# Four Flamingo-style gated layers on one core: x normalised once and turned by a diagonal product in the prelude, weight scales of the last layer folded into the weights

## The reference

```python
x = x + jnp.tanh(g_xattn[0]) * _L0_xattn_ref(_layernorm(x, axis=-1), ctx_4096, mask, ...)   # 32 heads of 128
x = x + jnp.tanh(g_ffn[0]) * _L0_ffn_ref(_layernorm(x, axis=-1), ...)
...
x = x + jnp.tanh(g_ffn[3]) * _L3_ffn_ref(_layernorm(x, axis=-1), ...)
```

```python
def _dynamic_quant(x, inv_smooth):
    xs = x.astype(jnp.float32) * inv_smooth
    scale = jnp.maximum(jnp.max(jnp.abs(xs), axis=-1, keepdims=True) / QMAX, 1e-08)
    return jnp.clip(jnp.round(xs / scale), -QMAX, QMAX), scale
qg, sg = _dynamic_quant(x_flat, inv_gate)      # x_flat is bf16, 1024 x 512
qu, su = _dynamic_quant(x_flat, inv_up)
gate_out = (qg @ w_gate.T) * sg * s_wgate[None, :]          # 256 columns
up_out = (qu @ w_up.T) * su * s_wup[None, :]
inter = jnp.clip(jax.nn.silu(gate_out) * up_out, -10, 10).astype(jnp.bfloat16)
qi, si = _dynamic_quant(inter, inv_inter)
out = (qi @ w_down.T) * si * s_wdown[None, :]
```

## Time and profile before

| what | value |
|---|---|
| three timed runs | 1664.83, 1665.88, 1668.33 us (median 1665.88) |
| the profiled execution | 1662.29 us, its span 1660.3 us |
| PE busy | 1584.1 us, 95% |
| DVE busy | 1004.5 us, 60% |
| ACT busy | 734.7 us, 44% |
| POOL busy | 411.3 us, 25% |
| mean granted clock of PE | 0.988 |

### The profile page before, as it was taken

How to read it: one execution, slowest core, us unless ns; L and a number is a source line. 1 busy time by engine, 2 the same in 40 slices (tenths; PEclk the granted TensorE clock), 3 DMA queues, 4 the chain that set the end, 5 groups by cost and what they waited for, 6 DMA issues and landing times.

```text
span 1660.3 us, 25939 instructions
## 1 busy us (share of the span) xinstructions
PE 1584.1 (95%) x8932; PEld 1266.5 (76%) x8932; DVE 1004.5 (60%) x2654; ACT 734.7 (44%) x2125; POOL 411.3 (25%) x271
## 2 busy tenths in 40 slices
PE   8899999999999999999989999999999999999875
PEld 6688888888888888888866869687876797655454
DVE  6763563626636265462876756657485767455787
ACT  4342443424434244442433544536272322677742
POOL 4231320313203132031215100000002533355452
PEclk9999999999999999999999999999999999999998
DMA  5110111101111111111242000000004213000001
GB/s 174 52 42 29 55 41 51 41 28 54 45 47 41 30 64 42 38 46 43 69 173 84 13 13 0 0 13 0 1 14 163 93 51 92 14 14 14 1 0 51
DMA packets 34145, 76.18 MB, mean 46 GB/s; under 512 B 5536, under 2 KB 18336, under 8 KB 31904
## 3 DMA queue, kind: packets, MB, share of 16 engines
q1 hardware_dynamic: 34080, 75.36, 13.5%
HBM read 73.25 MB, written 2.10 MB: 45 GB/s over the span
## 4 chain that ended last, share of the span: by engine, by line
PE 76%; DVE 13%; ACT 3%; issue 3%; DVEq 2%; POOL 1%; DMA 1%; POOLq 0%; SPq 0%; ACTq 0%
PE banks L1098 10%; PE banks L1023 9%; PE banks L1048 9%; PE banks L1031 9%; PE banks L1248 9%; PE banks L1352 5%; PE banks L1154 3%; PE banks L1137 3%; PE banks L1324 3%; PE banks L1476 2%; PE banks L1462 2%; PE banks L1144 2%; PE banks L1483 2%; PE banks L1455 2%; PE banks L1272 1%
## 5 line engine op out<-in xcount | busy, mean ns | idle before, releaser
L516 POOL TENSOR_TENSOR w_q<-w_raw_q,w_q 128x1792 fp32r<-128x1792 f32 x16 | 65.3, 4081 | 484.3 <-ACT w_q L706 484.3
L1098 PE MATMUL banks<-w_o,atT 128*128 128x512 f32 x720 | 180.2, 396 | 0.0
L1048 PE MATMUL banks<-w_v,cT 128*128 128x512 f32 x768 | 178.5, 393 | 0.0
L1023 PE MATMUL banks<-cT,w_k 128*128 128x512 f32 x720 | 178.0, 396 | 0.0
L1031 PE MATMUL banks<-xT,w_q 128*128 128x512 f32 x672 | 164.2, 395 | 5.4 <-DVE qT L1721 2.8
L1048 PEld LDWEIGHTS banks<-w_v,cT 128*128 128x128 f32 x768 | 145.4, 190 | 30.3
L1764 DVE TENSOR_TENSOR sA<-banks,pbias 128x512 f32<-128x512 f32 x64 | 44.1, 688 | 186.5 <-PE banks L1137 185.8
L1098 PEld LDWEIGHTS banks<-w_o,atT 128*128 128x128 f32 x720 | 132.0, 188 | 25.7
L1023 PEld LDWEIGHTS banks<-cT,w_k 128*128 128x128 f32 x720 | 131.9, 188 | 25.5
L1031 PEld LDWEIGHTS banks<-xT,w_q 128*128 128x128 f32 x672 | 123.6, 188 | 31.4 <-DVE qT L1721 3.2
L732 ACT ACTIVATE sA<-sA,nmA 128x128 f32<-128x128 f32 x256 | 99.5, 393 | 60.3 <-DVE nmA L1769 59.9
(11 more groups left out here) (266 smaller groups left out, 3291.2 us busy)
## 6 DMA issues: line engine op xcount, KB each, us to landing
w_raw_k<-in_w0k SPq DMA_DIRECT2D x16, 512.0 KB, 3.3
w_raw_v<-in_w0v SPq DMA_DIRECT2D x8, 1024.0 KB, 4.8
w_raw_q<-in_w0q SPq DMA_DIRECT2D x16, 512.0 KB, 3.3
w_raw_o<-in_w0o SPq DMA_DIRECT2D x15, 512.0 KB, 3.3
cTp<-in_ctxT SPq DMA_DIRECT2D x12, 512.0 KB, 4.0
wq_raw<-in_wq SPq DMA_DIRECT2D x1, 3072.0 KB, 11.3
wo<-in_wo SPq DMA_DIRECT2D x1, 3072.0 KB, 21.0
c_raw<-in_ctxT SPq DMA_DIRECT2D x4, 512.0 KB, 6.9
```

The source lines that it names most:

```text
L516: pool.tensor_tensor(w_part[slot][1][:], w_raw[slot][:], w_part[slot][0][:].bitcast(F32), ALU.subtract).then_inc(S(f"w{slot}_lo"), 1)
L1023: mm = pe.matmul(dst, wk_[l][:, c, h * P:(h + 1) * P], cT[r][:, c, half * HT:(half + 1) * HT], start=c == 0 and n == 0, stop=c == DC - 1 a ...
L1048: mm = pe.matmul(dst, cT[l][:, c, b * P:(b + 1) * P], wv_[r][:, c, :], start=n == 0, stop=n == 3 * DC - 1)
L1098: mm = pe.matmul(dst, atT[l][:, h, t], w[r][:, h, :], start=n == 0, stop=n == 5)
```

## The change

In the prelude:

- x_res is normalised in place, once, with `rstd` (the eight operations of L1675 write x_res, those of L1712 are gone). The further factor of the double norm, now `rr` = (var / (var + eps) + eps)^(-1/2), goes onto the diagonal of a 128 x 128 matrix for each block (`diag`, eight small operations on ACT, from POOL's `rr`), and `turn_x` multiplies the block by it instead of transposing it against the identity.
- There are three stage buffers for four blocks (the fourth takes the first one again), and POOL makes the low part of four operands, DVE of three.
- POOL waits for the eight normalisations before it splits w_q.
- The first keys start in smaller pieces: w_k's low part by quarters, the first chunk of the context by halves.

In the last feed-forward layer:

- The scales of the gate, up and down weights (sd3 with the gate in it) are multiplied into the weights themselves, by six POOL operations in the units 2 to 7 of pair 0 of the last attention layer. The sigmoid takes its input from PSUM with the row's scale, and DVE multiplies PSUM, scale and sigmoid in one operation each. `f3_gates` and its buffer are gone.
- The clip of the codes stands in `f3_round`, behind a drain, in place; `f3_clip` is gone. f3_turn(0) moves ahead of the last projection of the attention layer.
- The products add to x_res on DVE directly; `yd` and POOL's adds are gone.
- The hardware loops over the turns on PE, ACT and DVE are written out.

```diff
@@ SP
-            sp.wait_ge(S("x_split"), 2 * NPAIR)
+            sp.wait_ge(S("x_split"), NPAIR)
+            sp.wait_ge(S("x_split2"), NPAIR)
@@ POOL
-            split("k", 0)
+            pool.wait_ge(S("wk_hi"), 1)
+            for c in range(DC):
+                t = slice(c * 2 * P, (c + 1) * 2 * P)
+                pool.tensor_tensor(w_part["k"][1][:, t], w_raw["k"][:, t], w_part["k"][0][:, t].bitcast(F32),
+                                   ALU.subtract).then_inc(S("wk_lo"), 1)
             split("v", 0)
             pool.wait_ge(S("a_var"), 1)
+            pool.tensor_tensor(rstd[:], ve[:], neg_half[:], ALU.pow).then_inc(S("a_rstd"), 1)
+            pool.wait_ge(S("a_var"), 2)
             pool.tensor_tensor(rr[:], ms[:], neg_half[:], ALU.pow).then_inc(S("a_rstd"), 1)
-            pool.tensor_tensor(rstd[:], ve[:], neg_half[:], ALU.pow).then_inc(S("a_rstd"), 1)
+            pool.wait_ge(S("xr_ready"), NB)
             split("q", 0)
             for k in range(NPAIR):
                 t = slice(k * P, (k + 1) * P)
-                pool.wait_ge(S("x_hi"), k + 1)
-                pool.tensor_tensor(xT[1][:, XT1:, :, t], stage[k % 2][:, XT1:], xT[0][:, XT1:, :, t].bitcast(F32),
-                                   ALU.subtract).then_inc(S("x_split"), 1)
+                pool.wait_ge(S("x_prep"), NPAIR + k + 1)
+                pool.tensor_tensor(xT[1][:, X22:, :, t], stage[k][:, X22:], xT[0][:, X22:, :, t].bitcast(F32),
+                                   ALU.subtract).then_inc(S("x_split2"), 1)
...
+                if i == 0 and 2 <= u < 2 + DC + IC3:
+                    c = u - 2
+                    if c == 0:
+                        pool.wait_ge(S("f3_ws"), 1)
+                    if c < DC:
+                        pool.tensor_tensor(wg3[:, c, :], wg3[:, c, :], sgu3[:].rearrange("p w n -> p (w n)"), ALU.mult)
+                    else:
+                        pool.tensor_tensor(wd3[:, c - DC, :], wd3[:, c - DC, :], sd3[:], ALU.mult)
+                if i == 1 and u == 0:
+                    pool.drain().then_inc(S("f3_ws"), 1)
@@ ACT
+            def diagonal(k):
+                for b in (k, k + NPAIR):
+                    e = act.activation(diag[:, b, :], ident[:], ACT.Copy, scale=rr[:, b:b + 1])
+                e.then_inc(S("x_prep"), 1)
+
+            store_v(0, bank(0), K_UNITS + 1)
+            act.wait_ge(S("const_ready"), 1)
+            act.wait_ge(S("a_rstd"), 2)
+            diagonal(0)
+            store_v(1, bank(1), K_UNITS + 2)
+            for k in range(1, NPAIR):
+                diagonal(k)
...
-                    act.wait_ge(S("f3_g"), 2 * i + j + 1)
-                    act.activation(eg[:, j, :], gu[:, j, 0, :], ACT.Sigmoid).then_inc(S("f3_e"), 1)
+                    act.wait_ge(S("f3_gu"), 2 * i + j + 1)
+                    act.activation(eg[:, j, :], bank(4 + j)[:, 0:I3], ACT.Sigmoid, scale=xsc[:, i, j, 0:1])\
+                        .then_inc(S("f3_e"), 1)
@@ PE
             def turn_x(k):
                 for j, b in enumerate((k, k + NPAIR)):
+                    if j == 0:
+                        pe.wait_ge(S("x_prep"), k + 1)
                     pe.wait_ge(S("xr_ready"), 2 * k + j + 1)
                     if k > 0:
                         pe.wait_ge(S("xw_ready"), 3 * (k - 1) + j + 1)
                     for c in range(DC):
-                        mm = pe.transpose(bank(4 + j)[:, c * P:(c + 1) * P], xr[:, b, c * P:(c + 1) * P], ident[:])
+                        mm = pe.matmul(bank(4 + j)[:, c * P:(c + 1) * P], x_res[:, b, c * P:(c + 1) * P], diag[:, b, :],
+                                       start=True, stop=True)
                     mm.then_inc(S("xr_used"), 1)
...
+                f3_turn(0)
                 x3_project(NPAIR - 1, 1, 0, G3)
...
             def f3_gate_up(i):
-                if not (isinstance(i, int) and i == 0):
-                    pe.wait_ge(S("f3_g"), 2 * i)
-                for j in range(2):
+                for j in range(2):
+                    if i > 0:
+                        pe.wait_ge(S("f3_g"), 2 * i + j - 1)
@@ DVE
             for b in (b for k in range(NPAIR) for b in (k, k + NPAIR)):
-                dve.tensor_scalar(xr[:, b, :], x_res[:, b, :], mv[:, b, 0:1], rr[:, b:b + 1], ALU.subtract,
+                dve.tensor_scalar(x_res[:, b, :], x_res[:, b, :], mv[:, b, 0:1], rstd[:, b:b + 1], ALU.subtract,
                                   ALU.mult).then_inc(S("xr_ready"), 1)
...
             def rows_sums(k):
-                x = stage[k % 2]
-                if k >= 2:
-                    dve.wait_ge(S("x_split"), 2 * k - 1)
+                x = stage[k]
+                if k == NPAIR - 1:
+                    dve.wait_ge(S("x_split2"), 1)
...
-            dve.wait_ge(S("a_rstd"), 2)
-            for b in range(NB):
-                dve.tensor_scalar(x_res[:, b, :], x_res[:, b, :], mv[:, b, 0:1], rstd[:, b:b + 1], ALU.subtract, ALU.mult)
-            dve.drain()
...
                         dve.tensor_scalar(qs[:, i, j, w, :], xs[:, j, w, :], rsc[:, j, w:w + 1], ROUND, ALU.mult, ALU.add)
+                dve.drain()
+                for j in range(2):
+                    for w in range(2):
+                        dve.tensor_scalar(qs[:, i, j, w, :], qs[:, i, j, w, :], ROUND + QMAX, ROUND - QMAX, ALU.min, ALU.max)\
+                           .then_inc(S("f3_q"), 1)
...
             def f3_swiglu(i):
-                dve.wait_ge(S("f3_e"), 2 * i + 2)
-                dve.tensor_tensor(sg[:], eg[:], gu[:, :, 0, :], ALU.mult)
+                for j in range(2):
+                    dve.wait_ge(S("f3_e"), 2 * i + j + 1)
+                    dve.scalar_tensor_tensor(out=sg[:, j, :], in0=bank(4 + j)[:, 0:I3], scalar=xsc[:, i, j, 0:1],
+                                             in1=eg[:, j, :], op0=ALU.mult, op1=ALU.mult)
                 dve.drain()
-                dve.tensor_tensor(sg[:], sg[:], gu[:, :, 1, :], ALU.mult)
+                for j in range(2):
+                    dve.scalar_tensor_tensor(out=sg[:, j, :], in0=bank(4 + j)[:, I3:2 * I3], scalar=xsc[:, i, j, 1:2],
+                                             in1=sg[:, j, :], op0=ALU.mult, op1=ALU.mult).then_inc(S("f3_g"), 1)
                 dve.drain()
...
-                    dve.scalar_tensor_tensor(out=yd[:, j, :], in0=bank(6 + j), scalar=isc[:, i, j:j + 1], in1=sd3[:],
-                                             op0=ALU.mult, op1=ALU.mult).then_inc(S("f3_yd"), 1)
+                    dve.scalar_tensor_tensor(out=x_res[:, 2 * i + j, :], in0=bank(6 + j), scalar=isc[:, i, j:j + 1],
+                                             in1=x_res[:, 2 * i + j, :], op0=ALU.mult, op1=ALU.add).then_inc(S("res"), 1)
```

116 lines of the change are left out of this document (46 added, 70 removed).

## The result

The changed kernel took 1650.64 us (median of 4 runs, 1649.8 to 1654.09) beside 1666.34 us for the kernel before on the same chip (4 runs, 1664.83 to 1668.33): a ratio of 0.9909, 95% interval 0.9891 to 0.9927. It is faster by 0.9%, or 15.7 us, where 8.7 were forecast: at the lower end of the predicted range (1650 to 1664) and 6.6 us under the predicted time. The profiled execution took 1650.53 us with a span of 1648.8; that of before had a span of 1660.3.

The account below looks back on a forecast made before the run. TensorE (PE), busy 95% of the span, was taken as the bound, so only its idle time could yield gains. Prelude -2.9, x3 +2.9 and +1.7, f3 -10.4 gave -8.7 us: 1653.6, plus 3.6 carried over, 1657.2; range 1650 to 1664.

Parts of the forecast that it names:

- rival 1: f3: PE is the new bound, 8.74 us of work per turn; sum only -2.8, 1663.1 us; chance 0.08.
- rival 5: f3 runs at the lower clock throughout, two PE-bound turns cost about +13 us: 1670; chance 0.07.
- PE is full but for two gaps: Last attention layer (x3): PE idles only in gaps of 1.67 and 2.90 us, ended by a DVE copy.
- The weight products on POOL: x3, pair 0: six products, 7.6 us in all, have cover enough and cost 0; at worst +1.3 to +2 us.
- (c): Prelude pipeline: third buffer shortens the loop from 6.8 to 5.9 us per block; query products start 1.5 us earlier, near 55.6.
- Rival 3: Prelude: wider POOL block and w_q split hold DVE back, query products start at 57; gain 0, 1660.1 us; chance 0.08.
- The port: Prelude: DVE and POOL hold each other up without a semaphore; the third buffer notwithstanding, this keeps the pipeline in line.
- (d): Prelude: no second normalisation of x_res, so 42 query matmuls run without the 2.79 us wait, about 10.0 us; gain 3.1 us.
- (b): Prelude: turning x by a product instead of a transposition, +0.8 us per turn_x, +3.2 us of PE.
- rival 4: Prelude: turning by products costs four times a transposition, 4.1 us instead of 1.03; 1658.7 us; chance 0.05.
- The diagonals: Prelude: eight small ACT operations, about 0.3 us each by estimate, 2.4 us in all; first pair due at 26 us.
- Rival 2: The clock stays up at three new places (-3.4 us) and in f3's last down product; 1652 to 1653.8 us; chance 0.12.

Follow-up runs that it names:

- e8: e3 with ACT's sigmoid ahead of the copy of the codes and 11 identity products on TensorE before the last codes; 1643.39 us, ratio 0.9881.
- e5: The changed kernel with two stage buffers instead of three, its two separate counts kept; 1653.17 us (one run).
- e10: The kernel before with DVE's and POOL's splits of x counted by two semaphores instead of one; 1661.11 us (one run).
- e7: The kernel before with one wait more: POOL splits w_q only after DVE's eight normalisations; 1662.86 us (one run).
- e12: e9 with POOL's share of the split of x narrowed from 1024 to 768 columns and 11 identity products before the query products, not 18; 1637.46 us, ratio 0.9831.
- e6: The changed kernel with 18 identity products on TensorE in its idle time before the query products; 1648.31 us, ratio 0.9907.
- e1: The kernel before with the change's prelude edits alone; 1658.34 us, ratio 0.9963.
- e11: e10 with the wait of e7 as well; 1661.59 us (one run).
- e3: The changed kernel with the last two maxima, scales, rounding and clip of x3's pairs 0 and 1 moved behind the copy of y; 1644.35 us, ratio 0.9882.
- e9: The changed kernel with e3, e6 and e8 joined, 13 identity products at x3's start, four weight roundings moved out of the last pair; 1638.94 us, ratio 0.9837.

## Right and wrong, point by point

**f3, right, and 1.4 us better than its sum.** Predicted were swiglu(1) at 1619.8, swiglu(2) at 1627.0, swiglu(3) at 1635.7 behind a sigmoid that waits in ACT's queue, and codes at 1641.3. The rows say 1619.17, 1626.53, 1634.94 with `[1.46 <-ACT eg L982]` before it, 1640.08; the last down product ran at the lower clock as forecast. Chain, order of queues and sizes held. e8 then showed that ACT's order delayed the last sigmoid as the reading said (1.2 us). How much each edit of f3 (gates, clip, POOL's additions, the loops written out) is worth by itself is read from the rows; no run takes them apart. PE as the bound (rival 1) didn't come: of the loop's three turns only one, that of 1629.58, has no idle time ahead of gate and up, as the schedule had it. Nor did rival 5: the lower clock reached only the end.

**x3, the gaps right, the clock right only on average.** +4.6 predicted; the profiled pair shows +3.2, and over all kernels that have the changed stage as it is (196.8, 197.4, 196.9, 196.8) and that of before (193.7, 192.6, 192.9, 191.8, 193.9) the means are 197.0 and 193.0, +4.0. The gaps came out at 3.18 and 4.42 (predicted 3.1 and 4.35), +3.0 for +2.9, with the lower clock behind the first. But the stage as a whole held 20.5 us of lower clock before and 17.1 in the changed kernel, so in the profiled pair the clock took 1.7 us off where +1.7 was forecast; over the same two groups of kernels it is 17.9 and 15.0 us, which comes to +1.5. The other 1.9 us of the +3.2 aren't taken apart; `f3_turn(0)`, 1.97 us of PE's work, now stands inside the stage, where PE waited 0.82 us. The reading that PE is full but for two gaps was wrong: before also has 3.32 us at the start of the stage, 1.92 us at another copy of y (1493.29) and 6.3 us in the last pair, where 10.2 of the 20.5 us of lower clock lie. The weight products on POOL (1.26 to 1.45 us each) cost nothing that a row shows.

**Prelude, the sum right, its reason wrong.** Predicted -2.9, shown -2.9 at x3 (-3.2 to the scores). The step that failed is (c): "the third buffer takes the turning out of this loop". e5 shows it to be worth nothing once the counts are separate, e10 that separate counts in the kernel before give the same 3.1 us to the scores without it, e7 that the wait of POOL gives 1.0. The 6.8 us loop of before held a wait of 2.51 us for POOL that its own timeline shows; I worked out the loop's length and not what ended DVE's idle time in it. The new sum (DVE 1.77, ACT 1.70, POOL 2.41) gave 5.9, and 5.8 is right, because the chain really goes through POOL: a block's own sums are held up by POOL's operation on the block ahead. That this chain is longer than it need be (5.28 with the narrower share, e10 and e12) I took as given. Rival 3 had that half: the wider block holds DVE back, by 2 us until the query products, but not so far that they start at 57.

The port (the way into SBUF that DVE and POOL share by the prediction): on this the row and the Trainium skill (SBUF — State Buffer, Who interferes with whom) agree. It says that a DVE operation with two inputs in SBUF and a GpSimd operation that reads SBUF exclude each other for a whole instruction, whoever was first; L1718 took 2.34 and 2.31 us beside POOL's L516 and L534, and 0.42 alone.

The smaller terms: (d) the query products ran in one piece, 12.17 us at the lower clock and 10.12 in e6 at full clock, predicted 10.0 plus 1.7. (b) A turn costs 1.95 to 2.05 us against 1.03, twice and not four times, so rival 4 fell. The Trainium skill (TensorE: Matmul & The Clock Gate, Terms) has the transposing mode four times faster for FP32; here the rows give 1.9 to 2.0, and they decide. The diagonals took 0.29 us from one to the next, 1.86 for six, and PE waited 0.56 us for the first.

**The clock, right in its places.** The idle time ahead of the query products (4.62 us) and that at y (3.18 us) were followed by the lower clock, as forecast; e6 shows for the first of them that it goes when PE isn't idle. It took 6.8 us there, not 3.4, of which 4.4 fall on the products; it costs 2.0 us and not 1.7. Rival 2 (clock up at the new places) is out, though the measured time would have spoken for it: 1650.6 lies nearer to its 1652 to 1653.8 than to the forecast. The rows decide here, not the number.

**Basis, the rest of the 6.6 us.** The sum was -8.7; the profiled executions say -11.8 (1662.29 to 1650.53; in spans -11.5). That is 3.1 us, of which x3 and f3 have 1.4 each. To the sum I added 3.6 us, by which the profiled execution of before lay under the median of three runs. The changed kernel's profiled execution (1650.53) lies at its median (1650.64), so that was 3.5 us too much. These two misses have the same sign and carry the number to the edge of the range. For the 3.6 the runs show a cause: before's runs spread from 1661.62 to 1668.67 us over all sessions, and their mean granted clock goes with them (0.989 at 1661.62, 0.984 at 1668.51). A clock lower by 0.005 over 1660 us is 8.3 us of full-speed time, by estimate; these two runs differ by 6.9. The profiled execution, at 0.988, was a lucky one: its f3 took 55.1 us, with one stretch of 3.4 us of lower clock before the last turn; four other kernels with the same f3 (e1, e7, e10, e11) took 56.8 to 57.2, each with 10.2 us of it from about 1606 us on. Against these the f3 of the changed kernel gains 13.6 to 13.9, and that is 2 of the 4 us by which the medians (-15.7) and the spans (-11.5) differ. Where the other 2 us lie is open, since the timed runs leave only their span and mean clock. Some of it wanders: a stretch of 3.4 to 6.8 us near 835 to 850 us is there in e3, e6, e9, e10, e11 and e12 and not in the others, and e5 has one of 6.8 us at 1321 us.

## What to carry to other kernels

When an engine waits in a loop for a semaphore to which two engines add, check which increments can be there at that moment: a count meant as "both are done with block k-2" can mean "the other one is done with block k-1", and the idle time's releaser in the timeline says so before any buffer is added. In an engine's queue, whatever a third party doesn't wait for belongs behind the operation for which TensorE stands waiting; in e3 moving 4.9 us of maxima, rounding and clip (two times) behind a copy took 6.9 us out of the stage. And a sum made against one profiled execution carries its luck with the clock: compare its mean granted clock with those of the timed runs before carrying an offset over.
